# A first batch with its own orders: q and k rows of the first head group made by TensorE in place, the other heads behind the first scores, weight columns laid out by the host

## The reference

```python
def kernel_func(q, k):                                   # H = 16 heads of HD = 8
    scores = einsum('bhqd,bhkd->bhqk', q, k) / sqrt(HD)
    w = relu(scores)
    return w / (sum(w, axis=-1) + KERN_EPS)
# _L0_attn_ref: q, k, v from (x @ w_qkv).reshape(B, S, H, 3 * HD)
#   out = kernel_func(q, k) @ v;  y = x + out @ w_out + b_out;  layer norm of y, * gamma + beta
# _L0_ffn_ref: h = layer norm of x, * ln_gamma + ln_beta;  silu(h @ w1 + fc1_bias) @ w2 + fc2_bias
#   w1, w2 dequantised as (q - 128) * scales;  returns x + 0.5 * z
x = x + 0.5 * _L0_ffn_ref(_layernorm(x), ...)
x = x + _L0_attn_ref(_layernorm(x), ...)
x = x + 0.5 * _L0_ffn_ref(_layernorm(x), ...)
```

## Time and profile before

| | us |
|---|---|
| timed runs, median of 3 | 378.31 |
| lowest, highest | 377.96, 379.72 |
| profiled execution, in all | 380.02 |
| its span in the trace | 378.2 |
| TensorE busy in the span | 367.0 |
| VectorE, ScalarE, GpSimd busy | 289.7, 226.4, 217.5 |

### The profile page before, as it was taken

How to read it: one execution, slowest core, us unless ns; L and a number is a source line. 1 busy time by engine, 2 the same in 40 slices (tenths; PEclk the granted TensorE clock), 3 DMA queues, 4 the chain that set the end, 5 groups by cost and what they waited for, 6 DMA issues and landing times.

```text
span 378.2 us, 11736 instructions
## 1 busy us (share of the span) xinstructions
PE 367.0 (97%) x4586; PEld 190.6 (50%) x4586; DVE 289.7 (77%) x698; ACT 226.4 (60%) x414; POOL 217.5 (58%) x448
## 2 busy tenths in 40 slices
PE   8889998999999999999999999999999999999996
PEld 8764423353564445553554445653464444533486
DVE  4846777897778978787778978788776976886684
ACT  2357465667847577566857486566857576365503
POOL 7365085538963589437982589438881566146051
PEclk9999999999999999999999999999999999999999
DMA  6036005500351005400261005400270005400001
GB/s 167 29 85 170 3 0 118 135 3 2 89 137 59 1 10 148 126 3 0 68 160 59 0 2 134 122 29 0 53 174 30 2 2 133 120 3 1 2 2 60
DMA packets 14551, 23.05 MB, mean 61 GB/s; under 512 B 2720, under 2 KB 4256, under 8 KB 14496
## 3 DMA queue, kind: packets, MB, share of 16 engines
q1 hardware_dynamic: 11600, 17.70, 19.1%
q10 hardware_dynamic: 2896, 4.59, 3.8%
HBM read 3.41 MB, written 2.10 MB: 15 GB/s over the span
## 4 chain that ended last, share of the span: by engine, by line
PE 89%; DVE 5%; DMA 2%; ACT 1%; issue 1%; POOL 0%; ACTq 0%; SPq 0%; POOLq 0%; DVEq 0%
PE o_bank L490 30%; PE scores L475 16%; PE pre_bank L431 9%; PE post_bank L431 9%; PE pre_bank L436 4%; PE o_bank L412 3%; PE pre_bank L437 2%; PE post_bank L436 2%; DMA q_op<-q_parts 2%; PE pre_bank L424 2%; DVE probs L1048 2%; PE post_bank L450 2%; PE pre_bank L450 2%; PE post_bank L437 2%; PE post_bank L424 1%
## 5 line engine op out<-in xcount | busy, mean ns | idle before, releaser
L1048 DVE TENSOR_SCALAR probs<-scores 128x512 f32<-128x512 f32 x256 | 163.8, 681 | 48.0 <-PE scores L475 46.2
L764 ACT ACTIVATE probs<-scores 128x512 f32<-128x512 f32 x256 | 138.6, 596 | 67.5 <-PE scores L475 67.5
L490 PE MATMUL o_bank<-probs,v_op 128*32 128x512 f32 x1024 | 135.8, 603 | 0.0
L475 PE MATMUL scores<-q_op,k_op 32*128 32x512 f32 x512 | 76.0, 494 | 1.5 <-DMA q_op<-q_parts 1.3
L475 PEld LDWEIGHTS scores<-q_op,k_op 32*128 32x128 f32 x512 | 31.3, 181 | 83.5 <-issue 48.6
L654 ACT ACTIVATE pre_y<-pre_bank,b_sum,col_consts 128x512 f32<-128x512 f32 x28 | 21.8, 780 | 26.0 <-PE pre_bank L450 25.8
L490 PEld LDWEIGHTS o_bank<-probs,v_op 128*32 128x32 f32 x1024 | 21.6, 108 | 29.1 <-issue 23.5
L431 PE MATMUL pre_bank<-w,pre_y 128*32 128x128 f32 x960 | 30.9, 274 | 0.3 <-DVE w L798 0.3
L431 PEld LDWEIGHTS pre_bank<-w,pre_y 128*32 128x32 f32 x960 | 25.6, 110 | 8.3 <-issue 7.8
L431 PE MATMUL post_bank<-w,post_y 128*32 128x128 f32 x960 | 29.5, 273 | 0.0
L431 PEld LDWEIGHTS post_bank<-w,post_y 128*32 128x32 f32 x960 | 26.1, 110 | 6.0 <-issue 5.7
(11 more groups left out here) (190 smaller groups left out, 548.4 us busy)
## 6 DMA issues: line engine op xcount, KB each, us to landing
k_op<-k_parts SPq DMA_DIRECT2D x62, 128.0 KB, 2.6
q_op<-q_parts SPq DMA_DIRECT2D x62, 128.0 KB, 2.7
pre_x<-in_L_attn_x_dram ACTq DMA_DIRECT2D x7, 256.0 KB, 2.7
out_dram<-o_rows ACTq DMA_DIRECT2D x7, 256.0 KB, 2.0
w_int<-in_L_ffn_fc_q_dram SPq DMA_DIRECT2D x2, 256.0 KB, 3.9
rows<-in_lines_dram ACTq DMA_DIRECT2D x1, 256.0 KB, 5.4
s_rows<-in_L_ffn_fc_scales_dram SPq DMA_DIRECT2D x1, 256.0 KB, 6.2
q_op<-q_parts ACTq DMA_DIRECT2D x2, 128.0 KB, 2.8
```

What stands on the lines that cost most here:

```text
L475: mm(scores[i][:, j, :], k_op[rows, g, P * kt:P * (kt + 1)], q_op[rows, g, :], start=True, stop=True).then_inc(scores_done[i], 1)
L490: last = mm(o_bank[pair][VW * j:VW * (j + 1), :], v_op[:, kt, heads_of(g).start + 2 * j, :], probs[:, s % 2, j, :], start=(odd == 0 and kt ...
L764: activation(probs[:, s % 2, j, :], scores[0][:, j, :], ACT.Relu).then_inc(probs_done[0], 1)
L1048: v.tensor_scalar(probs[:, s % 2, 2 + j, :], scores[1][:, j, :], 0.0, None, ALU.max).then_inc(probs_done[1], 1)
```

## The change

Six things, all but the last two in the first batch alone.

1. Group 0's q and k rows of batch 0 aren't copied by DMA. The host lays out w_q and w_k also "by slot": the columns of group 0's 32 rows repeated for the four slots. TensorE multiplies with these (`k0`, `q0`, in halves of the tokens), so that all 128 rows stand in PSUM, ScalarE makes the high part with a sign and scale by partition (`sign_slot`) and VectorE writes q_op and k_op from it, with a factor by partition (`low_slot`), which leaves in each slot the part that belongs there. VectorE builds the two columns at the start (`prepare_slots`).
2. The rest of k and q (`first.k.1`, `first.q.1`, all heads, 512 tokens at once) comes behind the scores of steps 0 and 1, in o_bank1 and post_bank, and SP copies groups 1 to 3 from there on. The second half of v moves behind the scores of step 0. The fills of the first batch are counted by FIRST_FILLS.
3. GpSimd puts group 0's values in by halves (`first.v_in.0`, `first.v_in.1`).
4. Batch 0's steps have tables of their own (PE_START, ACT_START, DVE_START, POOL_START): hT of batch 1 comes in step 1, its fc1 in steps 3 to 6, its fc2 in steps 7 and 8. The FIRST lists are reordered, with 8 filler matmuls in place of 12, b1 ahead of hT.0, batch 1's x statistics ahead of x1.0, and the fillers around hT of batch 1 gone.
5. The host lays out w_qk, w_v and w_out; VectorE's sorting copies and seven of eight w_out DMAs go.
6. x has two buffers in the pre stage; SP loads batch 1's at the start, and batch b's load waits for batch b-2's readers.

```diff
+FIRST_FILLS = ["hT", "fc1.0", "fc1.1", "fc1.2", "fc1.3", "fc2", "uT", "v", "k", "q"]
+FIRST_PARTS = [("k0", 0), ("q0", 0), ("q0", 1), ("k0", 1)]
...
 PE_FIRST = [
...
+    "warm_up.8", "weights.b1", "first.hT.0", "first.fc1.0.0", "first.fc1.1.0", "first.hT.1", "first.low.0.0",
...
+PE_START = [
+    (["first.v.1", "first.k.1"], []),
+    (["first.q.1"], ["pre.hT@1"]),
+    ([], []),
+    (["pre.fc1.0@1"], []),
...
+    (["pre.fc2.0@1"], ["pre.fc2.1@1"]),
+    (["pre.fc2.2@1", "pre.fc2.3@1"], []),
+    ([], []),
+    ([], []),
+    ([], ["pre.uT@1"]),
...
+POOL_START = [
+    "post.u_bias", "v_in.2", "pre.x_stats@2", "v_in.3", "pre.x1_stats@1", "pre.u_apply@1", "pre.uT@1", "pre.x_apply@2",
+    "v_in.0@1", "v_in.1@1", "pre.x1_beta@1", "pre.xr@2"
 ]
...
@@ def step_scores
-                    pe.wait_ge(*emptied(pre, 1, "q"))
-                if kt == 0:
-                    pe.wait_ge(qk_in[g], 64 * (b + 1))
-                if b == 0 and s == 1:
-                    pe.wait_ge(keys_in, 32)
+                    pe.wait_ge(first_in, 3)
+                if b == 0 and s == TT // 2:
+                    pe.wait_ge(first_in, 4)
+                if kt == 0 and copied(g, b) > 0:
+                    pe.wait_ge(qk_in[g], copied(g, b))
...
@@ TensorE, edge
+                elif what in ("q0", "k0"):
+                    i = "qk".index(what[0])
+                    pe.wait_ge(wqkv_ready, 1)
+
+                    pe.wait_ge(*emptied(pre, 1, "fc1.3"))
+                    pe.wait_ge(b1_ready, 1)
+                    pe.wait_ge(*of_half(u_hi_a, u_hi_in, h, b))
+                    two_products(first_bank(i, h), wqk_hi[:, 2 + i, :], wqk_lo[:, 2 + i, :], pre.t_hi[:, cols])
+                    pe.wait_ge(*of_half(u_lo_a, u_lo_in, h, b))
+                    mm(first_bank(i, h), wqk_hi[:, 2 + i, :], pre.t_lo[:, cols], start=False, stop=True).then_inc(first_made, 1)
...
@@ ScalarE, edge
+                elif what in ("q0", "k0"):
+                    i = "qk".index(what[0])
+                    act.wait_ge(slots_ready, 2)
+                    act.wait_ge(first_made, FIRST_PARTS.index((what, h)) + 1)
+                    activation(first_high(i)[:, cols], first_bank(i, h), ACT.Copy, scale=sign_slot[:, i:i + 1]
+                               ).then_inc(first_high_in, 1)
...
@@ VectorE, edge
+                elif what in ("q0", "k0"):
+
+                    i = "qk".index(what[0])
+                    dve.wait_ge(slots_ready, 3)
+                    dve.wait_ge(first_high_in, FIRST_PARTS.index((what, h)) + 1)
+                    v.scalar_tensor_tensor((q_op, k_op)[i][:, 0, cols], first_bank(i, h), low_slot[:, i:i + 1],
+                                           first_high(i)[:, cols].bitcast(F32), ALU.mult, ALU.subtract).then_inc(first_in, 1)
...
@@ GpSimd
+            def first_values(h):
+
+                pool.wait_ge(v_ready, 3)
+                pool.wait_ge(*emptied(pre, h, "v"))
+                values(0, rows_in(h)).then_inc(v_in if h else v_in_a, 1)
...
@@ SP, the start
-                (w_raw[:, :], w_qkv, wqkv_loaded),
+                (wqk[:, :, :], w_qk.rearrange("p (i n) -> p i n", i=4), wqkv_loaded),
+                (wv[:, :], w_v, wv_loaded),
...
+            sp.dma_start(pre.x(1)[:, :, :], x_rows[1]).then_inc(x_loaded[1], 16)
+            sp.dma_start(wo[:, :], w_out).then_inc(wo_loaded, 16)
```

More of the change, by code:

```diff
@@ L172, in tasks, with build @@
             yield stage, what, batch
-def build(nc, x, w_qkv, w_out, fc1_q, fc2_q, fc2_scales, columns, lines, out):
+def build(nc, x, w_qk, w_v, w_out, fc1_q, fc2_q, fc2_scales, columns, lines, out):
     x_rows = x.rearrange("b (p t) d -> b p t d", t=TT)
@@ L758, in _ @@
             for b in range(B):
-                for s, beside in enumerate(ACT_ORDER):
+                for s, beside in enumerate(ACT_ORDER if b > 0 else ACT_START):
                     if STEPS * b + s - 1 > 0:
@@ L1219, in work @@
                         mix(norm_x2, tb)
+                    elif what.startswith("v_in"):
+                        first_values(int(what[-1]))
                     elif stage in ("first", "last"):
@@ L1226, in _ @@
             work(0, POOL_FIRST)
-            for b in range(B):
+            work(0, POOL_START)
+            for b in range(1, B):
                 for beside in POOL_ORDER:
```

287 lines of the change are left out of this document (176 added, 111 removed).

## The result

| | median us | lowest, highest | runs |
|---|---|---|---|
| before | 378.21 | 377.78, 379.72 | 6 |
| after | 381.48 | 380.14, 382.53 | 6 |

The changed kernel takes 1.0068 of the time before, 95% interval 1.0044 to 1.0091. It is slower by 3.3 us (2.6 by the ratio), where 0.9 us faster was forecast; the time lies outside the range. Two executions among all that follow are left out of the ratios as slow ones: one of before (543.74 us at a mean clock of 0.559) and one of e14 (385.21 us).

What follows compares the result with a forecast made beforehand. TensorE (busy 97%) bounds the batch loop, so time could be won only before the first scores: 5.45 us there, less 2.89 of moved work and added waits, left 0.9, so 378.31 became 377.4; range 375.7 to 379.2.

Steps and rivals of the forecast that it cites:

- The ruler: Gain read against marks of a profiled execution (380.02 us), then taken from the median of 378.31.
- Part 1, fc1 at 7.13: First batch's start: with fewer warm-ups and b1 ahead of hT.0, fc1 starts at 7.13 instead of 7.77.
- Part 1, x1 at 13.4: First residual sum on VectorE starts at 13.4 instead of 14.71, 1.3 us earlier.
- Their cover: Batch 1's statistics (1.2 us) ahead of x1 on VectorE fit into the wait for the Silus, otherwise costing 1.2.
- Part 1, the clock: TensorE's start: fewer warm-ups cost nothing, since the 2.4 GHz level was read as coming only from 7.97 on.
- second rival: Clock rises only after fc1: x1 1.0 us later, gain gone, 378.3; chance 0.14.
- The prediction's own sign: Forecast is wrong if 256-column products on TensorE are still spaced 0.20 us at 9 us.
- Part 2, x1 to the first scores: Without the DMA trip the first scores start at 21.05 instead of 26.51, 5.45 us won.
- Part 3, moved work 2.89: v.1, k.1, q.1 and batch 1's hT move behind TensorE's first scores and cost 2.89 us, unhidden.
- rival 3: DMA copies for group 1 land late, scores of step 4 wait: up to 380.3; chance 0.06.
- Part 3, waits: Between first scores and uT of batch 1: waits of 3.7 us, including 0.7 for hT and 1.2 for u.
- Rival 1: TensorE's waits for hT and u are absent, so 2.5 us are gained: 375.8; chance 0.25.

Runs made afterwards that it cites:

- e14: The changed kernel with more filler matmuls in the gaps of the front: 381.16 us, ratio to before 1.0067.
- e13: The kernel before, unchanged, one execution for a profile near its median: 378.02 us.
- e17: The changed kernel with the old start (12 fillers, hT.0 ahead of b1), front fillers and 10 passes ahead of uT of batch 1: 380.11 us, ratio 1.0045.
- e9: The changed kernel, unchanged, run a third time: 381.45 us, ratio to before 1.0069.
- e8: The kernel before without its 18 filler passes around hT of batch 1 (22.4 to 26.5 us): 381.52 us, ratio 1.0081.
- e4: The changed kernel with the statistics of batch 1's x1 a step earlier on VectorE: 379.07 us, ratio to before 1.0017.
- e5: The changed kernel with the old start and batch 1's x1 statistics a step earlier: 377.99 us, ratio to before 0.9986.
- e15: The kernel of e12 with more filler matmuls in the front: 377.42 us, ratio to before 0.9964.
- e1: The changed kernel, unchanged, run again: 382.27 us, ratio to before 1.0097.
- e7: The changed kernel with 10 filler passes just ahead of uT of batch 1: 379.98 us, ratio to before 1.0046.
- e10: The kernel of e7 run again: 381.77 us, ratio to before 1.0054.
- e3: The kernel before with the change's start (8 fillers, b1 ahead of hT.0): 380.30 us, ratio to before 1.0041.
- e12: e5's kernel with batch 1's x statistics behind uT.0's low half and ScalarE's hT copy ahead of step 2's probs: 377.34 us, ratio to before 0.9954.
- e16: The kernel of e12 run again on another chip: 377.37 us, ratio to before 0.9963.
- e6: The kernel of e5 with more filler matmuls in the front: 378.35 us, ratio to before 1.0008.
- e11: The kernel of e5 run again: 378.37 us, ratio to before 0.9976.
- e18: e17 with batch 1's x1 statistics a step earlier in place of the 10 passes ahead of uT: 379.01 us, ratio to before 1.0009.

## Why the prediction was wrong

Four terms of the sum failed: the clock, which got nothing and cost some 1.2 us (an estimate); x1, which had no wait for GpSimd's product and came 0.9 late; the waits behind the first scores, 0.5 too small; and the profile from which the gain was read, 0.7 too late in its marks. The first turned a small loss into a clear one, the others alone had turned the gain into a loss. The work that moved behind the scores was priced right.

Marks, beside the forecast. In the first two columns and in e14 the clock rose by the start of fc1 and didn't fall; in the last it rose at 11 us. e14 is the change with fillers behind fc2, so its x1 is that of the change:

| | before, record | before, e13 | forecast | after, e14 | after, record |
|---|---|---|---|---|---|
| fc1 starts | 7.77 | 7.27 | 7.13 | 7.54 | 8.37 |
| x1 | 14.71 | 14.21 | 13.4 | 14.27 | 15.56 |
| first scores | 26.51 | 25.79 | 21.05 | 22.11 | 23.40 |
| uT of batch 1 | 51.80 | 51.08 | 51.0 | 52.61 | 53.91 |

The forecast had a gain of 0.8 at uT; the clean comparison has a loss of 1.5. The 2.3 us between them are 0.7 of a wrong ruler, 0.9 at x1, 0.2 from there to the scores and 0.5 behind them. A further 0.2 is in no mark: an execution of the change takes 2.0 us more than its span, one of before 1.8. What then lies between 1.7 (e17) and 2.9 (the three ratios' mean, 1.0078) I put down to the clock, some 1.2 us. It is a difference between chips with intervals that overlap (1.0029 to 1.0060 against 1.0043 to 1.0094 for e9), so its size is an estimate; that a late rise and falls cost time is shown by marks (x1 1.1 to 2.3 us later) and by e8.

**The ruler.** "Waits and work are the same in both, so I take the difference from the median" was wrong. The profile took 1.7 us more than the median and had its own reasons for it: a rise of the clock 0.5 later than in e13 and 0.2 at the DMA in the front, 1.3 of waits in batch 1. Gains read against its marks were 0.7 too large.

**Part 1, fc1 at 7.13.** Only with an early rise, and then in part: 7.25, 7.36 and 7.54 in e4, e9 and e14, 8.0 to 8.4 where the level stayed low, 7.27 and 7.77 in the two profiles of before. The old start isn't fixed either: with it fc1 starts between 7.26 (e5) and 8.13 (e15), as the 24 passes take 4.3 to 5.5 us. hT.0, which had stood beside the wait for w1, now stands behind b1, and its copy by ScalarE is exposed (fc1.0 waits 0.47 for it in the profile after and in e14's).

**Part 1, x1 at 13.4.** Failed by 0.9, on VectorE's side, which I had as the one that just keeps up. VectorE was free for xr at 11.7 in e14, as forecast (11.6); but xr waited for GpSimd's product until 12.5 (0.78 in e14, up to 1.23 elsewhere), a step that my sum didn't have. In the profile of before the same product was there at 11.1, and in the change's first too:

```profile
9.40 1.75 POOL L1248 TENSOR_SCALAR pre_xr<-pre_x,norm_x_mix 128x128 f32<-128x128 f32 x4
```

In e14 it started at the same time and took 3.04 us instead of 1.75. Over the profiles its length goes with when VectorE starts on w2 and the 512-column casts: 1.75 where w2 starts 1.4 us behind it (both first profiles, e1, e7; in e10 2.05), 1.94 at 1.0 (e8), 2.46 and 2.51 at 0.8 and 0.9 (e13, e3), 2.9 to 3.1 where w2 starts within 0.6 us or ahead of it (the twelve others). So the product is longer the more of that work runs beside it, and the change, which brings the work forward, takes part of its own gain. No run was made to separate the two, so the cause isn't shown beyond this.

With xr at 12.5 the statistics of batch 1 end at 14.25, and x1 follows at once (14.06 to 14.39, in all profiles with an early rise and the statistics ahead of it). "Their cover is the wait for the Silus; without it they would cost 1.2": the cover was there for half of them. In e12, e15 and e16 fc1's start to x1 is 5.99 us, so x1 could have come at 13.53 in e14; the statistics cost 0.74 there, and so does the long product, since with xr at 11.7 they would have fitted (an estimate from these rows). The cast of 512 columns took 0.42 (0.5 assumed).

**Part 1, the clock.** "By my reading nothing" was the worst sentence. Its price stood in the second rival (x1 1.0 later; the four late profiles have it 1.1 to 2.3 later than e14's), with a chance of 0.14 where four of the eight profiles with the new start had it (the change's first, e1, e7 and e10) and none of the twelve with the old one. The prediction's own sign, products still spaced 0.20 at 9 us, is what the profile after shows. The reading itself was wrong: I took 0.20 between the first two products for the 1.2 GHz level. In e13 the first pair is 0.20 apart too with all others at 0.12; at the lower level the first pair is 0.38 apart (8.37, 8.75) and the rest 0.21. So in the earlier trace rows the clock was up by 7.77, behind 24 passes and hT.0 without a pause, which the change cut.

**Falls of the clock.** No rival had them. The change fills the front with short products that wait for other engines, drops the 18 passes at 22 to 26 us, and adds the wait for u; each stood in the text as work or wait and nowhere as what the clock sees. The Trainium skill (TensorE: Matmul & The Clock Gate, "HAM oscillation — how this bites in real kernels") describes waits that take the clock down again and again; e8 shows one such case with its price, 2.9 us for two waits of 3.1 together.

**Part 2, x1 to the first scores.** Right: 7.65 forecast, 7.61 in e5, 7.84 in e12 and e14. The scaled half copy takes 0.47 to 0.48, the upper bound (0.43 assumed), but successive ones start 0.36 apart, so the row of four costs no more. The DMA trip's 3.7 us are the whole gain: 25.79 to 22.11 is 3.7, and x1 gave none.

**Part 3, moved work 2.89.** Right: v.1 0.58, k.1 and q.1 0.89 each, hT 0.58, 2.94 in all. Group 1's copies land in time: rival 3 is out.

**Part 3, waits.** fc1.0's wait was 0.46 (0.7 forecast), u's 1.28 (1.2). First scores to uT took 30.50 in e14, 5.2 more than the 25.29 of both profiles of before; less 2.9 of work that is 2.3 more waiting, where 1.8 was forecast. Near enough, and it shows that the sum had no slack: of 3.7 won, 2.9 went to moved work and 2.3 to waits. Rival 1 (waits absent, 375.8) had the right lever and the wrong size, since taking u's wait away gives 1.1.

**The range.** 375.7 to 379.2 held e4, e5, e6, e11, e12, e15, e16 and e18, versions with something mended, and not the change. "Slower" had 0.07 since its rival was a DMA; the two causes at work, clock and x1's other inputs, were in the text with no part in it.

## What to carry to other kernels

Before an early phase is shortened, list what TensorE does in each stretch of it: fillers that stand in a wait may be holding its clock for the work behind, and a phase with less waiting but small gaps can run at half the clock. Take marks from a profile near the median, not from the one at hand. When the last input of a step is moved earlier, name the second-last and when it is there; here it was a GpSimd product at 12.5, and work put into the "free" time cost 0.74 of its 1.2 us. Check too what a step that is moved runs beside: that product took 1.75 us with little beside it and 3.04 beside VectorE's work. Moving two statistics and one copy and keeping the old start turned the loss of 0.7 to 1.0% into a gain of 0.4% (e12, e16).
